# One store of eight PSUM banks, and turns by the chain of work left, in an eight-row transformer stack

## The chip, the cores and the metric

The kernel runs on one NeuronCore of a Trainium2 chip. The metric is the device time of one execution in microseconds (us), the median of several runs. The engines are TensorE (PE; its weight loads are listed as PEld), VectorE (DVE), ScalarE (ACT), GpSimd (POOL) and SyncE (SP), which issues most DMAs. PSUM is the memory that PE writes its results to, and DVE and ACT read from; it has eight banks of 512 float32 values in each of its 128 partitions.

## The reference, cut to what matters

Eight independent batch rows x[8, 256, 128] pass through four layers, each a gated attention followed by a gated feed-forward, with layer normalisation ahead of both:

```python
x = x + tanh(g_xattn[l]) * xattn_l(layernorm(x), ctx)    # l = 0..3, 256 x 256 attention
x = x + tanh(g_ffn[l])   * ffn_l(layernorm(x))
# attention l = 0, 1, 3: 16 heads of 8;  l = 2: 4 heads of 32 over one key/value head
#   l = 0 adds adj[256,256] and a mask, l = 1 has rms norms, rope and a causal mask
# ffn 0: one of 8 experts a token, 128x128;  ffn 1: 128 -> 512 -> 128 with low-rank experts, top 2
# ffn 2: one of 8 experts, 128 -> 512 with gelu, then 512 -> 128, layernorm
# ffn 3: only the tokens of rows 0 and 1 are fed (128 -> 1024 -> 128)
```

## The kernel before, in words

**Rows and lines.** The work of one batch row is cut into about 180 steps such as `("max", l, row, p)`, listed by `row_steps`. A step may have a part on several engines, in a fixed order (its `phases`). Four rows are in work at once. There are four lines: line b runs row b and then row b + 4, in order, and the four lines share all engines.

**The planner.** `Plan.place` runs on the host when the kernel is built. It walks through time with a table of durations (`COST`, with `HOP` from engine to engine and `LANDS` for DMAs) and writes out one order for each engine (`plan.orders`), which the engine then follows strictly. Whenever an engine is free, each line offers its next step on it, if what it depends on (`starts_after`) and the buffers it takes (`takes`, `psum_uses`) are there; of those that could start now, the one with the smallest `turn_of` is put next. Before, `turn_of` is the step's number in its row less the `HEAD_START` of the row: 740, 850, 700 and 699 for rows 0 to 3; 5, 40, 14 and 0 for rows 4 to 7. So every step of rows 0 to 3 goes ahead of every step of rows 4 to 7, and row 1 keeps ahead of row 0 until it is 110 steps further on.

**PSUM.** Seven banks are a common store (`BANKS`): a step takes one bank ("one") or two neighbouring ones ("two") when PE starts it, and gives them back when DVE or ACT has read them. The order says which earlier use each bank had, and PE waits for that reader's semaphore (`claim`). The eighth bank, `pv`, stands apart: it holds the weighed values of one row's attention.

**One attention.** For the wide layers (l = 0, 1, 3) eight `max` steps compute scores for row maxima: PE fills two banks, DVE reduces them (L1423; L1418 for the half-wide ones). The maxima are turned on PE (`shift_flip`, L1088), copied by ACT and sent by DMA as extra rows beside the queries. Then eight `attend` steps compute the transposed scores in two banks, DVE adds the bias in layer 0 (L1442), ACT takes exp into one of four `probs` buffers (L921, L926), POOL masks in layer 1 (L812), and after each two of them a `weigh` step multiplies the values by them into `pv` (16 PE instructions in a wide layer: float32 takes two a product). `divide` is ACT's copy of `pv` to memory (L930, its semaphore is `sums`); `o_flip` and `mix` follow (L1453 to L1461). Nearly all products are issued from one helper, L969; transposes of stacked queries and keys from L665.

**One turn.** A ring "turn" of one entry lets only one row at a time be between its first `attend` and its `sums`, in the plan; on the chip ACT's placing of the values for the attention waits for the former row's `sums` (`turn_before`), and so does PE in the first `weigh`.

Of the kernel before, what the change touches and what calls it, by code (L numbers as in the profile page):

```python
# [12 lines left out]
F32 = mybir.dt.float32  # L13
# [8 lines left out]
P = 128  # L22
BATCH = 8
# [17 lines left out]
SUBLAYERS = 8  # L41
TAIL_ROWS = 2
GROUP = 8
STACKS, WIDES, PROBS, BANKS = 3, 2, 4, 7
COLS = 32
LANES = P // COLS
SETS = HEADS // LANES
# [79 lines left out]


AHEAD = 2
HEAD_START = [740, 850, 700, 699, 5, 40, 14, 0]  # L130


COST = {"load": [("SP", .4), ("PE", .4), ("ACT", .27), ("DVE", 1.55), ("POOL", .7)], "mask": [("SP", .4)], "fetch": [("SP", .8)], "consts": [("SP", 3)],
# [29 lines left out]
LANDS = {"consts": CONSTS, "load": 4, "mask": 4, "fetch": 4, "shift_flip": 3.4, "store": 2}  # L163
HOP = {"PE": .32, "DVE": .14, "ACT": .16, "POOL": .12, "SP": .1}
# [3 lines left out]
def phases(s):  # L168

    own = COST.get(s[:2], COST[s[0]])  # L170
    if s[0] == "attend" and s[1] != 2 and s[3] == 0:
        own = [(e, us + PLACING) if e == "ACT" else (e, us) for e, us in own]
    return own
# [71 lines left out]
def takes(s, eng):  # L245

    kind, l, row = s[:3]
    out = []
    if eng == "PE":
        out += [(use, ring, until) for use, ring, until in psum_uses(s)]  # L250
    if kind == "attend" and eng == ("DVE" if l == 0 else "ACT"):
        out.append(("probs_in", "probs", ("weighed", l, row, s[3] // 2)))
    if kind == "attend" and eng == "PE" and s[3] == 0:
        out.append(("turn", "turn", ("sums", l, row)))
    if (kind, eng) == ("mask", "SP"):
        out.append(("mask", "wide", ("biasT_ps", 0, row)))
    if (kind, l, eng) in (("spread", 0, "DVE"), ("spread", 2, "DVE"), ("inner", 1, "ACT")):
        out.append(("wide", "wide", ("f_ps", l, row)))
    if (kind, eng) == ("deep", "ACT") and s[3] == 0:
        out.append(("wide", "wide", ("f_ps", 3, row)))  # L260
    if eng == "ACT" and ((kind in ("kv", "query") and l in (0, 3)) or kind in ("k_turn", "q_turn")):
        out.append((f"{kind[0]}s", "stack", (f"{kind[0]}T_ps", l, row, 1)))
    return out
# [63 lines left out]
class Plan:  # L327


    def __init__(self, rings):  # L330
# [9 lines left out]
                    self.value[(stage, *s[1:])] = count[stage]  # L340
        self.names = sorted(count)

    def place(self):

        lines = [[] for _ in range(ROWS)]
        for b in range(ROWS):
            held = None
            for row in range(b, BATCH, ROWS):
                begin, rest = row_steps(row)
# [8 lines left out]
        lines = [[s for s in line if s[0] != "next"] for line in lines]  # L358
# [4 lines left out]
        ended = {}  # L363
        slots = {ring: [0.0] * n for ring, n in self.rings.items()}
        pending, former = {}, {}
        rank = {s: b for b, line in enumerate(lines) for s in line}
        step = {}
        for row in range(BATCH):
            begin, rest = row_steps(row)
            step.update({s: n for n, s in enumerate(begin + rest)})  # L370

        def turn_of(s):

            return (step.get(s, 0) - HEAD_START[s[2]], s[2])


        def fits(ring, t=None):
# [43 lines left out]
        while todo:  # L421
            best = None
            for eng in ENGINES:
                ready = []
                for b in range(ROWS):
                    q = queues[eng, b]
                    if at[eng, b] < len(q):
                        t = earliest(q[at[eng, b]], eng)
                        if t is not None:
                            ready.append((t, q[at[eng, b]]))  # L430
                if ready:
                    now = max(clear[eng], min(t for t, _ in ready))
                    t, s = min(((t, s) for t, s in ready if t <= now), key=lambda c: turn_of(c[1]))
                    if best is None or now < best[0]:
                        best = (now, eng, s)
            now, eng, s = best
            b = rank[s]
            at[eng, b] += 1
            todo -= 1
            self.orders[eng].append(s)  # L440
            clear[eng] = ended[s, eng] = end = now + dict(phases(s))[eng]
            for use, ring, until in takes(s, eng):
                got = fits(ring, now)
                bank = "one" if ring == "two" else ring
                self.home[(use, *s[1:])] = (ring, got[0])
                self.freed_by[(use, *s[1:])] = [former[bank, i] for i in got if (bank, i) in former]
                for i in got:
                    slots[bank][i] = None
                    former[bank, i] = until
                    pending.setdefault(until, []).append((bank, i))  # L450
            for stage in signals(s, eng):
                for bank, i in pending.pop((stage, *s[1:]), []):
                    slots[bank][i] = end + HOP[eng]
# [3 lines left out]
def build(nc, dram, out):  # L457
    plan = Plan({"one": BANKS, "probs": PROBS, "wide": WIDES, "stack": STACKS, "turn": 1})

    with ExitStack() as ctx:  # L460
# [102 lines left out]
        small, rest = (t[0:3 * E, :, :].rearrange("p r n -> p (r n)") for t in (probs[2], probs[1]))  # L563

        banks = ctx.enter_context(nc.psum_tensor("banks", [P, BANKS * 512], F32))
        pv = ctx.enter_context(nc.psum_tensor("pv", [P, 512], F32))


        const_in = ctx.enter_context(nc.semaphore("const_in"))
# [7 lines left out]
        sem = {}  # L577
# [36 lines left out]
        def turn_before(l, row):  # L614

            ended = [t for t in plan.orders["ACT"] if t[0] == "divide"]
            i = ended.index(("divide", l, row))
            return ("sums", *ended[i - 1][1:]) if i else None
# [4 lines left out]
        def programs(block):  # L623
            def at(stage, s):
                return plan.value[(stage, *s[1:])]

            def bank(use, s):
                ring, i = plan.home[(use, *s[1:])]
                return banks[:, i * 512:(i + (2 if ring == "two" else 1)) * 512]

            def claim(eng, use, s):

                for stage in plan.freed_by[(use, *s[1:])]:
                    eng.wait_ge(sem[stage[0]], plan.value[stage])
# [193 lines left out]
            def _(act):  # L828
# [8 lines left out]
                for s in plan.orders["ACT"]:  # L837
                    kind, l, row = s[:3]
# [88 lines left out]
                                           scale=1.0 if l == 2 else HD ** -0.5).then_inc(sem["probs"], 1)  # L927
                    if kind == "divide":
                        act.wait_ge(sem["weighed"], at("weighed", ("weigh", l, row, SETS - 1 if l != 2 else 0)))
                        act.activation(weighed_sb[b][:, :, :], pv[:, :].rearrange("p (g q) -> p g q", g=2), ACT.Copy).then_inc(sem["sums"], 1)  # L930
                    if kind == "route" and l == 1:
                        act.wait_ge(sem["gate_in"], at("gate_in", s))
# [31 lines left out]
            def _(pe):  # L964
# [6 lines left out]
                for s in plan.orders["PE"]:  # L971
# [137 lines left out]
                    if kind == "weigh":  # L1109

                        part = s[3]
                        if part == 0:
                            if l == 2:
                                pe.wait_ge(sem["v"], at("v", ("kv", l, row)))
                            else:
                                pe.wait_ge(sem["v_placed"], at("v_placed", ("attend", l, row, 0)))
                            ended = turn_before(l, row)
                            if ended:
                                pe.wait_ge(sem[ended[0]], plan.value[ended])
                        g, j = part // 2, part % 2  # L1120
                        both = [("attend", l, row, 2 * part + i) for i in range(2)]
                        ready = "masked" if l == 1 else "probs"
# [519 lines left out]
```

## Time and profile before

| | us |
|---|---|
| median of 3 runs (lowest, highest) | 1163.98 (1162.83, 1172.91) |
| the profiled execution | 1158.67 |
| its span, first to last instruction | 1156.9 |
| PE busy / DVE busy / ACT busy / POOL busy | 938.3 / 794.3 / 501.8 / 302.9 |
| mean granted clock of TensorE | 0.838 |

The busy time of an engine is the time in which it has an instruction in work. The granted clock is a share of 2.4 GHz; its two levels in this trace are 1.0 (2.4 GHz) and 0.5 (1.2 GHz). A row of the waits says which engine and line sat idle, which instruction's semaphore ended that, for how long in all, how often, and the longest. PE takes its instructions in the written order: while it waits, all that is behind waits too.

### The profile page before, as it was taken

To read this page: it belongs to the slowest core of one execution; us is meant where nothing else is said; L and a number is where in the kernel's file an instruction comes from. 1 tells how busy PE (TensorE), PEld (TensorE's weight loads), DVE (VectorE), ACT (ScalarE), POOL (GpSimd) and SP (SyncE) were. 2 spreads that over 40 slices of the span, in tenths; PEclk is the share of its full clock that TensorE was granted. 3 is DMA by queue.
4 is the path that set the end of the run, shared out by engine and by line. 5 is a ranking of instruction groups with operands and counts; after the bars stand their busy time and mean duration, and the time that the engine had idled before them with its cause. 6 is when DMAs were issued, how large, how long until landed. Compare 5 with 4: busy or idle time off the path is not lost.

```text
span 1156.9 us, 19280 instructions
## 1 busy us (share of the span) xinstructions
PE 938.3 (81%) x7316; PEld 592.9 (51%) x7316; DVE 794.3 (69%) x1849; ACT 501.8 (43%) x760; POOL 302.9 (26%) x324
## 2 busy tenths in 40 slices
PE   4787677698998889888975887887887898998776
PEld 3442335364564467555753452355554666666533
DVE  5889888848626844856099489999786747744473
ACT  3563354352325433364082835553454234353056
POOL 3520405343123003301031221245443314010000
PEclk7787788776779889778986998797998989699969
DMA  8000000000000000000000000000000000000000
GB/s 313 15 1 2 2 2 1 1 2 1 1 2 2 2 6 11 8 2 6 1 29 2 20 19 2 1 2 1 1 4 1 1 1 2 2 1 6 0 2 16
DMA packets 11741, 14.26 MB, mean 12 GB/s; under 512 B 1604, under 2 KB 10716, under 8 KB 11396
## 3 DMA queue, kind: packets, MB, share of 16 engines
q1 hardware_dynamic: 11552, 12.88, 3.4%
q8 instruction: 61, 1.00, 0.4%
q10 hardware_dynamic: 100, 0.14, 0.1%
q14 instruction: 28, 0.23, 0.1%
HBM read 11.55 MB, written 1.05 MB: 11 GB/s over the span
## 4 chain that ended last, share of the span: by engine, by line
PE 49%; DVE 35%; ACT 8%; issue 5%; POOL 2%; DMA 1%; SPq 0%; ACTq 0%; DVEq 0%
PE banks L969 37%; DVE nm_row L1423 10%; PE pv L969 7%; DVE probs L1442 3%; PE banks L665 2%; DVE qf_row L1453 2%; ACT probs L926 2%; DVE wide L1512 2%; DVE st_row L1266 2%; DVE xn_row L1378 2%; DVE mv_row L1268 1%; POOL kss_row L759 1%; ACT qT_row L843 1%; PE banks L1023 1%; ACT probs L921 1%
## 5 line engine op out<-in xcount | busy, mean ns | idle before, releaser
L1423 DVE TENSOR_REDUCE nm_row<-banks 128x4 f32<-128x1024 f32 (+1 forms) x192 | 209.4, 1126 | 38.5 <-PE banks L969 38.0
L759 POOL TENSOR_TENSOR rstd_row<-rstd_row,neghalf 128x2 f32<-128x2 f32 x66 | 47.2, 716 | 413.4 <-DVE rstd_row L1373 297.3
L926 ACT ACTIVATE probs<-banks 128x1024 f32<-128x1024 f32 (+1 forms) x144 | 126.4, 929 | 53.4 <-PE banks L969 52.1
L969 PE MATMUL pv<-probs,vpad 128*32 128x256 f32 (+1 forms) x1536 | 111.8, 414 | 23.6 <-ACT probs L921 11.1
L969 PE MATMUL banks<-kT_row,qT_row 48*128 48x256 bf16 (+2 forms) x896 | 103.4, 328 | 32.5 <-DVE nm_row L1423 18.6
L969 PE MATMUL banks<-wide,c 128*128 128x256 f32 x512 | 126.1, 402 | 0.0
L969 PE MATMUL banks<-qT_row,kT_row 50*128 50x256 bf16 (+2 forms) x896 | 98.8, 331 | 31.6 <-ACT probs L926 7.7
L969 PEld LDWEIGHTS banks<-wide,c 128*128 128x128 f32 x512 | 99.7, 200 | 17.8 <-issue 0.7
L969 PEld LDWEIGHTS banks<-kT_row,qT_row 48*128 48x128 bf16 (+1 forms) x896 | 42.5, 121 | 100.0 <-issue 52.9
L921 ACT ACTIVATE probs<-probs 128x1024 f32<-128x1024 f32 x64 | 67.2, 1055 | 55.5 <-DVE probs L1442 53.8
L969 PEld LDWEIGHTS banks<-qT_row,kT_row 50*128 50x128 bf16 (+1 forms) x896 | 49.1, 124 | 77.4 <-issue 21.3
L969 PEld LDWEIGHTS pv<-probs,vpad 128*32 128x32 f32 x1536 | 46.8, 119 | 66.9 <-issue 34.5
L1442 DVE TENSOR_TENSOR probs<-banks,biasT_row 128x1024 f32<-128x1024 f32 x64 | 75.9, 1217 | 5.9 <-PE banks L969 5.0
L665 PE MATMUL banks<-identb,stack 128*128 128x128 bf16 x768 | 65.1, 248 | 16.6 <-DVE stack L1412 13.6
L759 POOL TENSOR_TENSOR kss_row<-kss_row,neghalf 128x32 f32<-128x32 f32 x8 | 44.4, 5544 | 116.5 <-DVE kss_row L649 116.4
L969 PE MATMUL banks<-c,wide 128*128 128x128 f32 x512 | 73.5, 304 | 0.6 <-POOL wide L817 0.6
L665 PEld LDWEIGHTS banks<-identb,stack 128*128 128x128 bf16 x768 | 55.1, 113 | 29.9 <-DVE stack L1412 18.7
L969 PEld LDWEIGHTS banks<-c,wide 128*128 128x128 f32 x512 | 68.7, 215 | 3.0 <-ACT kT_row L843 0.8
L657 ACT ACTIVATE stack<-qf_row 128x768 bf16<-128x768 f32 x48 | 40.3, 843 | 58.8 <-DVE qf_row L1387 22.1
L1378 DVE TENSOR_SCALAR xn_row<-x_row,mv_row,rstd_row 128x128 f32<-128x128 f32 x116 | 49.7, 482 | 21.0 <-POOL rstd_row L759 12.7
L953 ACT ACTIVATE wide<-banks 128x1024 f32<-128x1024 f32 x8 | 8.2, 1025 | 126.3 <-PE banks L969 126.3
L812 POOL TENSOR_SCALAR_AFFINE_SELECT probs<-probs 128x512 f32<-128x512 f32 x64 | 41.0, 654 | 80.9 <-ACT probs L926 80.3
(221 smaller groups left out, 1646.6 us busy)
## 6 DMA issues: line engine op xcount, KB each, us to landing
c<-in_c SPq DMA_DIRECT2D x1, 2500.0 KB
wide<-in_mask SPq DMA_DIRECT2D x8, 256.0 KB, 3.2
qT_row<-mT_row SPq DMA_DIRECT2D x96, 4.0 KB
c<-in_c SPq DMA_DIRECT2D x1, 1194.5 KB
xn_row<-in_ctx SPq DMA_DIRECT2D x8, 128.0 KB, 3.5
x_row<-in_x SPq DMA_DIRECT2D x8, 128.0 KB, 2.9
late<-in_late SPq DMA_DIRECT2D x2, 512.0 KB, 14.8
out<-x_row SPq DMA_DIRECT2D x8, 128.0 KB, 1.9
```

The source lines that it names most:

```text
L657: return nc.scalar.activation(stack[:, :, lo:hi, :], heads(src)[:, :, None, :].to_broadcast([P, NT * HEADS, hi - lo, HD]), ACT.Copy)
L665: ins = pe.transpose(dst[:, jj * SEQ + t * P:jj * SEQ + (t + 1) * P], src[:, hh:hh + 2, :, :].rearrange("p h g d -> p (h g d)"), identb[:, :])
L759: return pool.tensor_tensor(t, t, neghalf[:, 0:n], ALU.pow)
L812: pool.affine_select(diag, diag, [[0, 2], [0, NT], [1, P]], ALU.is_ge, 0.0, base=0, channel_multiplier=-1).then_inc(sem["masked"], 1)
L921: act.activation(dst[:, :, :], dst[:, :, :], ACT.Exp).then_inc(sem["probs"], 1)
L926: act.activation(dst[:, :, 0:w], src[:, :, 0:w], ACT.Exp, scale=1.0 if l == 2 else HD ** -0.5).then_inc(sem["probs"], 1)
L969: return pe.matmul(dst, lhsT, rhs, start=start, stop=stop, **kw)
L1266: ch.link(V.bn_stats(sums[b][:, t, :], src[:, t, :]))
L1378: ins = V.tensor_scalar(xn[b][:, t, :], x[b][:, t, :], mv[b][:, t, 0:1], rstd[b][:, t:t + 1], ALU.subtract, ALU.mult)
L1423: V.tensor_reduce(nm[b][:, t, :, 2 * jp:2 * jp + 2], ps[:, :, :, 0:kn], AX.X, ALU.max, negate=True).then_inc(sem["max"], 1)
L1442: V.tensor_tensor(held(probs, "probs_in", s)[:, :, :], bank("scores_ps", s)[:, :].rearrange("p (r n) -> p r n", r=2), bt[:, None, :].to_br ...
L1453: ch.link(V.reciprocal(over, den))
```

## The change

The `pv` tensor is gone and `BANKS` is 8. The first `weigh` of an attention takes a bank of the common store as "one", held until `sums`; all its `weigh` steps and `divide` use that bank. In the first `weigh`, PE waits for the bank's earlier reader (`claim`) in place of the former row's `sums`. ACT's `turn_before` wait and the "turn" ring stay.

The planner's turns change too. `work_left` gives each phase of each step the length of the longest chain of work of the same row that hangs on it, by the same table; along an engine the steps of a line are chained in their order. An engine now takes, of what could start, the phase with the largest sum of chain left (us) and `LEAD` of its row. The order of all engines is planned anew; no instruction is added or taken away.

```diff
-STACKS, WIDES, PROBS, BANKS = 3, 2, 4, 7
+STACKS, WIDES, PROBS, BANKS = 3, 2, 4, 8
...
-HEAD_START = [740, 850, 700, 699, 5, 40, 14, 0]
+LEAD = [274.2, 264.8, 306.7, 298.2, 14.3, 5.0, 24.2, 33.5]
...
+    if kind == "weigh" and s[3] == 0:
+        out.append(("pv_ps", "one", ("sums", l, row)))
...
+    def work_left(self, lines):
+
+        left, after = {}, {}
+        for line in lines:
+            former = {}
+            for s in line:
+                for eng, _ in phases(s):
+                    ahead = [(o, e, HOP[e] + (LANDS.get(o[0], 0) if e == "SP" else 0)) for o, e in starts_after(s, eng)]
+                    if eng in former:
+                        ahead.append((former[eng], eng, 0))
+                    for o, e, lag in ahead:
+                        if o[2] == s[2]:
+                            after.setdefault((o, e), []).append((s, eng, lag))
+                    former[eng] = s
+        for line in lines:
+            for s in reversed(line):
+                for eng, us in reversed(phases(s)):
+                    left[s, eng] = us + max([lag + left[n, e] for n, e, lag in after.get((s, eng), [])], default=0)
+        return left
...
-        def turn_of(s):
-
-            return (step.get(s, 0) - HEAD_START[s[2]], s[2])
+        left = self.work_left(lines)
+
+        def turn_of(s, eng):
+
+            return (-left[s, eng] - LEAD[s[2]], s[2])
...
-        pv = ctx.enter_context(nc.psum_tensor("pv", [P, 512], F32))
...
+                        pv = bank("pv_ps", ("weigh", l, row, 0))
                         act.activation(weighed_sb[b][:, :, :], pv[:, :].rearrange("p (g q) -> p g q", g=2), ACT.Copy).then_inc(sem["sums"], 1)
...
-                            ended = turn_before(l, row)
-                            if ended:
-                                pe.wait_ge(sem[ended[0]], plan.value[ended])
+                            claim(pe, "pv_ps", s)
+                        pv = bank("pv_ps", ("weigh", l, row, 0))
```

## Rows read from the trace of the kernel before

**Rows 1.** The page: its span, and each engine's busy us, share and instructions.
```profile
span 1156.9 us, 19280 instructions
PE 938.3 (81%) x7316; PEld 592.9 (51%) x7316; DVE 794.3 (69%) x1849; ACT 501.8 (43%) x760; POOL 302.9 (26%) x324
```
**Rows 2.** The page: the chain that ended last, shares of the span by engine.
```profile
PE 49%; DVE 35%; ACT 8%; issue 5%; POOL 2%; DMA 1%; SPq 0%; ACTq 0%; DVEq 0%
```
**Rows 3.** Busy us of each engine by stretch; granted clock, DMA share, GB/s.
```profile
50.00:200.00 150.00, 112.44 (x974) 59.77 (x973) 131.18 (x246) 71.90 (x98) 42.67 (x26) 0.81 0.01 2
200.00:350.00 150.00, 128.35 (x873) 81.16 (x872) 90.32 (x246) 50.93 (x90) 49.52 (x54) 0.75 0.01 1
350.00:600.00 250.00, 211.79 (x1568) 146.83 (x1564) 146.92 (x375) 109.14 (x162) 49.03 (x68) 0.88 0.03 8
600.00:850.00 250.00, 199.28 (x1753) 112.58 (x1749) 212.04 (x450) 123.80 (x179) 87.94 (x67) 0.82 0.02 6
850.00:1050.00 200.00, 178.49 (x1327) 122.28 (x1320) 125.54 (x348) 83.90 (x144) 47.38 (x72) 0.89 0.01 2
1050.00:1157.00 107.00, 79.64 (x665) 50.23 (x663) 53.62 (x90) 41.52 (x54) 4.29 (x6) 0.86 0.02 6
```
**Rows 4.** Waits of PE: us in total, times, longest us; five of its groups.
```profile
PE banks L969 <- DVE nm_row L1423: 31.5, 53, 2.3
...
PE banks L969 <- ACT probs L926: 9.9, 19, 1.8
PE banks L969 <- DVE probs L1442: 9.4, 13, 2.5
...
PE banks L969 <- DVE qf_row L1365: 5.6, 2, 5.4
...
PE banks L969 <- DVE nm_row L1418: 2.5, 2, 1.9
```
**Rows 5.** Five short stretches of `max` steps, columns as in rows 3, and their sum.
```profile
36.50:46.50 10.00, 7.84 (x56) 2.79 (x55) 9.43 (x10) 2.13 (x6) 3.81 (x3) 1.00 0.11 34
...
613.00:628.00 15.00, 8.04 (x56) 3.33 (x57) 15.00 (x15) 0.23 (x1) 0.00 (x0) 0.65 0.01 1
...
sum 59.00, PE 43.83 PEld 16.07 DVE 56.50 ACT 12.70 POOL 3.81; mean PE 8.77 PEld 3.21 DVE 11.30 ACT 2.54 POOL 0.76
```
**Rows 6.** The page's groups: the reduction behind each `max` step, busy and mean ns.
```profile
L1423 DVE TENSOR_REDUCE nm_row<-banks 128x4 f32<-128x1024 f32 (+1 forms) x192 | 209.4, 1126 | 38.5 <-PE banks L969 38.0
```
**Rows 7.** The tile `pv`: its copy by ACT, and who waited for it.
```profile
L930 ACT ACTIVATE biasT_row<-pv x32: 597/597/618, 67.3 to 1149.0; 128x512 f32<-128x512 f32 x32
...
  ACT biasT_row L930: 48.1, 27
  DVE qf_row L1453: 25.8, 7
  PEld banks L969: 3.4, 6
  PE banks L969: 1.5, 3
```
**Rows 8.** Timeline of SP: the stores of rows 1, 5 and, last, three rows.
```profile
460.28 0.41 SPq L733 DMA_DIRECT2D out<-x_row  x1
...
1064.01 0.42 SPq L733 DMA_DIRECT2D out<-x_row  x1
...
1136.32 18.70 SPq L733 DMA_DIRECT2D out<-x_row  x3
```
**Rows 9.** Two stretches with PE nearly always busy, columns as in rows 3.
```profile
545.00:600.00 55.00, 49.13 (x317) 38.48 (x315) 22.77 (x52) 21.74 (x26) 5.88 (x7) 0.99 0.05 15
...
269.00:292.00 23.00, 21.74 (x109) 10.45 (x107) 19.83 (x57) 6.59 (x12) 5.43 (x3) 0.51 0.01 1
```

More of the change, by code:

```diff
@@ L366, in place @@
         rank = {s: b for b, line in enumerate(lines) for s in line}
[L367 to L370, printed above, removed]
-        def turn_of(s):
-            return (step.get(s, 0) - HEAD_START[s[2]], s[2])
+        left = self.work_left(lines)
+        def turn_of(s, eng):
+            return (-left[s, eng] - LEAD[s[2]], s[2])
         def fits(ring, t=None):
@@ L432, in place @@
                     now = max(clear[eng], min(t for t, _ in ready))
-                    t, s = min(((t, s) for t, s in ready if t <= now), key=lambda c: turn_of(c[1]))
+                    t, s = min(((t, s) for t, s in ready if t <= now), key=lambda c: turn_of(c[1], eng))
                     if best is None or now < best[0]:
```

## The prediction

> **What bounds the kernel now.** I read the page first. PE is busy for 938.3 us of 1156.9 and DVE for 794.3 [rows 1]; no other engine is near. PE is thus idle for 1156.9 - 938.3 = 218.6 us, and as the change neither adds nor takes away an instruction, it can gain only from these 218.6 us, or from PE's clock. The chain that ended last runs over PE for 49% of the span and over DVE for 35% [rows 2]: neither engine bounds alone. The busy time by stretch says when each does [rows 3]. From 50 to 200 us, when all four first rows are in their first layer, DVE is busy for 131.18 us of 150 (87%) and PE for 112.44 (75%). From 200 to 600 us PE leads, with 340.1 of 400 (85%). From 600 to 850 us, where rows of the second half begin, DVE is again ahead with 212.04 of 250 (85%) beside 199.28 (80%). From 850 to 1050 us PE is busy for 178.49 of 200 (89%, the best), and the last 107 us fall back to 79.64 (74%). So the kernel alternates between stretches set by DVE and stretches set by PE. A better order would put the PE work of one row beside the DVE work of another.
>
> The waits of PE tell what a bank is worth [rows 4]. PE fills banks that somebody must have read before. Five of its groups end with such a reader: 31.5 us for the reduction of the maxima (53 times), 9.9 for exp, 9.4 for the bias, 5.6 and 2.5 for two others, 58.9 us in all. Part of the 9.9 may be a wait for data, so I count 58.9 as the most that banks can cost PE by these rows.
>
> **Part 1, the eighth bank.** A wait for a bank has two possible causes: too few banks, or a reader that can't keep up. Five stretches of `max` steps, 59 us together, tell them apart: PE is busy for 43.83 us and DVE for 56.50 [rows 5]. PE is idle for 15.2 us of them, DVE for 2.5. In the one from 613 to 628 us DVE is busy for all 15.00 us and PE for 8.04. A reduction takes 1126 ns [rows 6] and PE has the next two banks full before that; with a fourth pair of banks PE gets ahead by one more step and then waits as before. What the bank takes away at once is at most DVE's own idle share, 2.5 of 15.2, which on the 58.9 us is 9.7 us. Beyond that, the step that PE runs ahead shortens a later stretch only if PE sets that one. There are 24 wide attentions; at one `max` step of PE each, worked out as 7.84 us of PE over 8 steps and other work [rows 5], so under 0.98 us, this is under 23.5 us, and I take an eighth of it, 3 us, since the bank is not free whenever values are being weighed and the next stretch is often DVE's. The term is -12.7 us, between 0 and -58.9.
>
> A rule speaks for more: the Trainium skill, Perfetto Trace Analysis, section Matmul Optimizations, says that all eight PSUM banks should be used so that instructions can overlap. Here all eight are used already, one of them for `pv` alone; the trace agrees with the rule only so far as the reader has time left. By the rule the term would be the whole -58.9 us, by the stretches above -9.7 us.
>
> **Part 2, the wait of the first `weigh`.** Removed: PE's wait for the former `sums`. No row of PE's waits has `pv` waiting for L930; the waits for that copy are ACT's own for its input and those of what reads the result [rows 7]. It stood behind the "turn", which stays. So nothing is gained. Added: a claim of one bank, 32 times. What is queued behind it is the `weigh` (16 matmuls) and then everything on PE. If no bank is read yet, the wait is up to one reduction, 1.126 us [rows 6], so 32 x 1.126 = 36 us at the worst. The plan starts the `weigh` only where it expects a bank, and three short waits are as much as I'd expect to go wrong: +2 us, between 0 and +36. The copy itself stays as it is, 32 times 597 ns [rows 7]. DMAs are unchanged in number; their issue moves with their steps, on a queue with nothing else to do.
>
> **Part 3, the order of turns.** The old order keeps row 1 far ahead: it is stored at 460.28 us and its line's second row, row 5, at 1064.01 us; the other three lines end together, with their stores between 1136.32 and 1155.0 us [rows 8]. So the last 93 us have three rows in place of four, and PE is idle for 27.4 us of the last 107 [rows 3]. The new order gives the turn to the longest chain left plus a lead. The leads of the first four rows differ by 42 us and those of the last four by 28.5, so the four lines are held within some 40 us of chain of each other, and all run nearly to the end. Suppose the last 107 us reached the idle share of the stretch before (21.5 of 200, 10.8%): 11.5 us idle, a gain of 15.9. But the end of any last row is a bare chain (exp, weigh, divide, spread, mix), and about half of the gain is lost to it: -8 us. In the middle, 600 to 850 us has 50.7 us of PE idle (20%). Begun together, the second rows would be like the first in 50 to 200 us, 25% idle; for 150 us that is 37.6 us against 30.4 at the present share: +7 us. In exchange the first rows finish together, none waits for its line, and the PE-heavy second layers of the feed-forward can be laid beside others' attention by chain length rather than by step number, which counts a step of 15 us in the planner's table like one of 0.4 us. I can't price this from a row; the bound is the difference between the idle share of the whole (218.6 of 1156.9, 18.9%) and the best stretch (10.8%), 8.1% of 1156.9 = 94 us below, and to the share of the first 150 us (25%), +71 us above. Between ends so far apart I take the sixth part of the gain way that a better measure of urgency may bring, -9 us, nearer to no change because DVE-set stretches stay. The sum of part 3 is -8 + 7 - 9 = -10 us.
>
> **The clock.** The mean grant is 0.838. The Trainium skill, TensorE: Matmul & The Clock Gate, section The HAM clock gate, ties 2.4 GHz to a busy PE, so a denser order would be rewarded. Here the rows disagree: from 545 to 600 us PE is busy for 49.13 of 55 at 0.99, but from 269 to 292 us it is busy for 21.74 of 23 at 0.51, the low level [rows 9]. So I price the clock at nothing. By the rule, with the cost of the low level at most 938.3 x (1 - 0.838) = 152 us and the idle time down by a tenth, it would be up to 15 us more gain.
>
> **Sum.** 1156.9 - 12.7 + 2 - 10 = 1136.2 us of span. The profiled execution was 1.8 us longer than its span, and the median of the runs is 5.3 us above the profiled one, so 1136.2 + 1.8 + 5.3 = 1143.3; I say 1142 us, 1.9% under 1163.98.
>
> **Rivals.**
> Rival A, banks are the bound: all 58.9 us of rows 4 go, with the order's -10: 1156.9 - 58.9 - 10 + 7.1 = 1095 us; a half of it still gives 1124. For it: waits for readers are a quarter of PE's idle time. Against: DVE is busy for 96% of the stretches where they fall.
> Rival B, nothing comes of it: what PE gets ahead is given back to DVE, whose 794.3 us lie in the same places, and the end is a bare chain anyhow. 1164 us, within 1% either way. For it: the two engines share the last chain nearly evenly.
> Rival C, lockstep, on the slower side: the lines kept within 40 us of chain bring all four rows to the same DVE-heavy layer at once, as in 50 to 200 us, and the far-ahead row 1 that now fills the gaps is lost. If the 25% idle share of that stretch holds for 250 us more than now, in place of 18.9%, the cost is 250 x 0.061 = 15 us; with no gain from part 1 the time is 1179 us. It decides once PE is idle for more than about 230 us in all. For it: the first 150 us are just this case. Against: the leads keep the rows some 10 us apart, and the "turn" forces a further distance.
> By these: my forecast 0.50, A 0.12, B 0.22, C 0.16. About 1% is what a measurement of this kernel can tell from no change; a tenth of my own case falls within it. Faster by over 1%: 0.45 + 0.12 = 0.57. Within 1%: 0.22 + 0.05 = 0.27. Slower by over 1%: 0.16. The range runs from a half of rival A with a little more from the order, 1110 us, to rival C's 1179; the forecast's own range is 1120 to 1155.
>
> **What the next profile would show.** Right: PE busy within some 15 us of 938 and its idle time near 198 us; the waits of PE for L1423 down by about a fifth, not gone, with DVE still near 96% busy in the `max` stretches; no noticeable wait of the first `weigh`; four stores in the last 40 us or so; PE busy above 80% in the last 107 us. A is right if waits for the readers fall below 20 us. C is right if the first 200 us and those around 600 us have PE under 75%. The forecast is wrong if PE's idle time stays at 219 us, if the mean clock moves by over 0.03 (it would outweigh part 1), or if banks taken one at a time by `weigh` split the pairs, so that waits of `max` and `attend` steps grow.

## The result, and the profile after

The changed kernel takes 1084.42 us (median of 4 runs, 1081.33 to 1086.0) where the kernel before took 1163.4 us beside it (4 runs). The ratio is 0.930, with a 95% interval of 0.925 to 0.936: 7.0% faster. The forecast was 1142 us with a range down to 1110; the direction was right, and the size was off by a factor of three and a half (79 us for 22).

The page of the changed kernel begins with its span and the busy time of each engine (us, share, instructions), as in [rows 1]:

```profile
span 1081.3 us, 19274 instructions
...
PE 887.4 (82%) x7316; PEld 572.0 (53%) x7316; DVE 793.3 (73%) x1849; ACT 493.2 (46%) x753; POOL 302.5 (28%) x324
```

PE has the same 7316 instructions, yet its busy time fell by 938.3 - 887.4 = 50.9 us. Its idle time fell from 218.6 to 1081.3 - 887.4 = 193.9 us, by 24.7. So of the 75.6 us of span two thirds came out of PE's busy time, which the prediction priced at nothing, and one third out of idle time, which is all that it priced. PE did not get less work: it is the clock, whose mean grant is 0.894 against 0.838. Busy time times mean grant, an estimate of the work in us at the full clock, is 786 us before and 793 after. The other executions agree: their grants are 0.875 to 0.894 for the changed kernel and 0.826 to 0.847 for the kernel before. With two levels, a mean of 0.838 puts PE at the low one for 32% of the span, 375 us; a mean of 0.894 is 21%, 229 us. DVE's busy time did not move (794.3 and 793.3 us).

Stretches of the changed kernel, with the columns of [rows 3] (busy us of PE, PEld, DVE, ACT, POOL; granted clock; DMA share; GB/s):

```profile
50.00:200.00 150.00, 119.61 (x998) 69.51 (x998) 137.06 (x276) 72.97 (x97) 43.22 (x25) 0.83 0.01 2
200.00:350.00 150.00, 126.81 (x1094) 80.49 (x1092) 112.95 (x301) 65.56 (x130) 63.96 (x76) 0.90 0.01 2
350.00:600.00 250.00, 223.92 (x1763) 151.52 (x1755) 165.53 (x377) 116.06 (x163) 43.66 (x57) 0.92 0.04 12
600.00:850.00 250.00, 197.16 (x1772) 116.75 (x1770) 212.40 (x504) 120.75 (x185) 97.13 (x87) 0.86 0.01 2
850.00:1050.00 200.00, 177.69 (x1303) 127.37 (x1301) 122.85 (x292) 79.08 (x122) 31.42 (x47) 0.92 0.01 2
...
974.30:1081.30 107.00, 81.53 (x767) 48.69 (x764) 64.48 (x105) 53.40 (x71) 4.19 (x6) 0.85 0.02 7
```

The reader should compare the first five stretch by stretch with [rows 3]. PE is busy for 119.6 us from 50 to 200 us, not 112.4, and the clock is higher in all five: 0.90 for 0.75 from 200 to 350 us, 0.92 for 0.88 and for 0.89 in the third and the fifth. From 600 to 850 us, where the second rows begin, DVE is still ahead with 212.4 us of 250. The last row is the last 107 us, as long as the last row of [rows 3]: PE is idle for 25.5 us of them, where it was 27.4.

SP's stores tell when each row ends, as in [rows 8]:

```profile
525.42 0.39 SPq L751 DMA_DIRECT2D out<-x_row  x1
536.66 0.41 SPq L751 DMA_DIRECT2D out<-x_row  x1
572.19 0.41 SPq L751 DMA_DIRECT2D out<-x_row  x1
595.97 0.42 SPq L751 DMA_DIRECT2D out<-x_row  x1
...
1048.68 10.62 SPq L751 DMA_DIRECT2D out<-x_row  x2
1069.02 10.36 SPq L751 DMA_DIRECT2D out<-x_row  x2
```

The first four rows end within 71 us of each other and are all out at 596 us; the last four are stored between 1048.7 and 1079.4 us. Before, one line ended at least 72 us ahead of the others.

Three of PE's waits for a bank's reader, as in [rows 4]:

```profile
PE banks L988 <- DVE nm_row L1441: 37.6, 56, 2.3
...
PE banks L988 <- DVE probs L1460: 12.2, 19, 1.1
...
PE banks L988 <- ACT probs L944: 9.4, 21, 1.0
```

They did not shrink, with one bank more: 59.2 us where the same three groups had 50.8.

And by shape, the float32 products of layer 2's attention, first of the kernel before, then of the changed one (count | busy us, mean ns | idle before them):

```profile
L969 PE MATMUL banks<-qT_row,kT_row 34*128 34x256 f32 x128 | 26.0, 561 | 0.5 <-DVE nm_row L1423 0.5
L969 PE MATMUL banks<-kT_row,qT_row 33*128 33x256 f32 x128 | 24.5, 525 | 3.1 <-DVE nm_row L1423 1.7 <-DVE nm_row L1418 0.7 <-ACT qT_row L896 0.4
...
L969 PE MATMUL pv<-probs,v_row 128*32 128x256 f32 x128 | 14.6, 540 | 2.6 <-ACT probs L926 2.6
```

```profile
L988 PE MATMUL banks<-qT_row,kT_row 34*128 34x256 f32 x128 | 17.8, 398 | 0.4 <-ACT kT_row L861 0.4
L988 PE MATMUL banks<-kT_row,qT_row 33*128 33x256 f32 x128 | 17.2, 391 | 0.0
...
L988 PE MATMUL banks<-probs,v_row 128*32 128x256 f32 x128 | 10.1, 384 | 1.1 <-ACT probs L944 0.8 <-issue 0.3
```

Same shapes, same counts, 540 ns before and 384 after: in the kernel before most of layer 2's attention ran at the low level, in the changed one next to none of it. The rows of these three groups are 20.0 us shorter together, beside the 50.9 us of all PE work.

### The profile page after: what moved, and what is told of

It reads as the page before. It is cut to its first block, busy times and chain, and to the rows that moved or that the text cites. A ratio compares the mean times of both kernels' runs of the same rounds, so it can differ in the third digit from the quotient of the medians.

```text
span 1081.3 us, 19274 instructions
## 1 busy us (share of the span) xinstructions
PE 887.4 (82%) x7316; PEld 572.0 (53%) x7316; DVE 793.3 (73%) x1849; ACT 493.2 (46%) x753; POOL 302.5 (28%) x324
## 4 chain that ended last, share of the span: by engine, by line
PE 45%; DVE 39%; ACT 7%; issue 6%; SPq 1%; DMA 1%; POOL 1%; DVEq 0%; ACTq 0%
PE banks L988 41%; DVE nm_row L1441 11%; DVE probs L1460 4%; ACT probs L944 3%; DVE wide L1530 2%; PE banks L683 2%; DVE qf_row L1471 2%; DVE st_row L1284 2%; DVE mv_row L1286 1%; DMA xn_row<-in_ctx 1%; DVE xn_row L1396 1%; DVE oh_row L1506 1%; DVE stack L1430 1%; DVE qr_row L1426 1%; PE banks L1042 1%
## 5 line engine op out<-in xcount | busy, mean ns | idle before, releaser
L1441 DVE TENSOR_REDUCE nm_row<-banks 128x4 f32<-128x1024 f32 (+1 forms) x192 | 211.8, 1129 | 55.5 <-PE banks L988 55.0
L988 PE MATMUL banks<-probs,vpad 128*32 128x256 f32 (+1 forms) x1536 | 108.1, 402 | 14.0 <-ACT probs L939 7.0
L988 PE MATMUL banks<-qT_row,kT_row 50*128 50x256 bf16 (+2 forms) x896 | 90.1, 300 | 29.1 <-DVE nm_row L1441 13.6
L988 PE MATMUL banks<-kT_row,qT_row 48*128 48x256 bf16 (+2 forms) x896 | 95.0, 303 | 19.1 <-DVE nm_row L1441 12.6
L988 PE MATMUL banks<-c,wide 128*128 128x128 f32 x512 | 78.6, 317 | 2.7 <-POOL wide L835 2.3
L988 PEld LDWEIGHTS banks<-kT_row,qT_row 48*128 48x128 bf16 (+1 forms) x896 | 37.2, 110 | 82.1 <-issue 49.8
L988 PEld LDWEIGHTS banks<-qT_row,kT_row 50*128 50x128 bf16 (+1 forms) x896 | 40.8, 110 | 71.9 <-issue 30.1
L988 PEld LDWEIGHTS banks<-c,wide 128*128 128x128 f32 x512 | 72.6, 226 | 7.2 <-issue 4.9
L988 PEld LDWEIGHTS banks<-probs,vpad 128*32 128x32 f32 x1536 | 45.8, 116 | 55.0 <-issue 26.2
L683 PEld LDWEIGHTS banks<-identb,stack 128*128 128x128 bf16 x768 | 52.8, 109 | 25.0 <-DVE stack L1430 14.7
L861 ACT ACTIVATE qT_row<-banks 128x1024 bf16<-128x1024 bf16 x48 | 47.4, 1022 | 31.9 <-PE banks L683 31.5
```

The costliest lines, as they stand in the source:

```text
L683: ins = pe.transpose(dst[:, jj * SEQ + t * P:jj * SEQ + (t + 1) * P], src[:, hh:hh + 2, :, :].rearrange("p h g d -> p (h g d)"), identb[:, :])
L861: act.activation(dst, cols, ACT.Copy, **kw).then_inc(sem[stage], 1)
L988: return pe.matmul(dst, lhsT, rhs, start=start, stop=stop, **kw)
L1441: V.tensor_reduce(nm[b][:, t, :, 2 * jp:2 * jp + 2], ps[:, :, :, 0:kn], AX.X, ALU.max, negate=True).then_inc(sem["max"], 1)
```

## The experiments

The change has two parts, the bank and the turns, and the second has three things in it: the measure (chain left in place of step number), the spread of the four rows (near even in place of one far ahead), and the choice of one set of eight numbers, which settles one order among many. Theory T says that the turns made the gain, theory S the bank. Each kernel builds its orders with the planner in it; that planner's own end is quoted with each run. It is the figure of a table, not a measurement, and the last of the tables below sets it beside the chip. Only the lines of an edit that matter are shown; `...` stands for what is left out.

### The two parts alone: e1 and e2

e1 is the changed kernel with the old turns:

```diff
-LEAD = [274.2, 264.8, 306.7, 298.2, 14.3, 5.0, 24.2, 33.5]
+HEAD_START = [740, 850, 700, 699, 5, 40, 14, 0]
...
-            return (-left[s, eng] - LEAD[s[2]], s[2])
+            return (step.get(s, 0) - HEAD_START[s[2]], s[2])
```

> The eight-bank store alone; turns by step number with the old leads. Theory T (the turns made the gain): no change, 1150 to 1172 us, PE idle about 215 us and granted clock about 0.84. Theory S (the bank made it, rival A of the prediction): at least half of the 79 us, so under 1124 us. The kernel's planner, by its own table, ends at 1078.7 us where the kernel before has 1077.0.

e2 is the kernel before with the new turns, `pv` apart and seven banks:

```diff
-HEAD_START = [740, 850, 700, 699, 5, 40, 14, 0]
+LEAD = [274.2, 264.8, 306.7, 298.2, 14.3, 5.0, 24.2, 33.5]
...
-            return (step.get(s, 0) - HEAD_START[s[2]], s[2])
+            return (-left[s, eng] - LEAD[s[2]], s[2])
```

> Turns by the chain left plus the new leads, pv apart and seven banks as before. Theory T: at least three quarters of the 79 us, so under 1105 us, with the clock near 0.89. Theory S: over 1124 us. A third, that each needs the other (a bank pays only when rows are close together), expects something between, and e1 without gain. The planner ends at 1049.5 us, against 1017.3 for the changed kernel.

e1 took 1153.8 us, 0.995 of the kernel before (0.992 to 0.997). e2 took 1115.6 us, 0.958 (0.953 to 0.963). Their busy times:

```profile
span 1151.3 us, 19281 instructions
...
PE 930.8 (81%) x7316; PEld 597.7 (52%) x7316; DVE 794.0 (69%) x1849; ACT 501.3 (44%) x761; POOL 302.6 (26%) x324
```

```profile
span 1123.9 us, 19277 instructions
...
PE 916.7 (82%) x7316; PEld 582.1 (52%) x7316; DVE 789.1 (70%) x1849; ACT 501.7 (45%) x757; POOL 303.1 (27%) x324
```

The bank alone is worth about 7.5 us under the old turns (0.3 to 0.8%); S falls. None of it shows as idle time in the profiled executions: PE is idle for 1151.3 - 930.8 = 220.5 us in e1, against 218.6 before, and its waits for the three readers did not fall but rose, from 50.8 to 68.7 us:

```profile
PE banks L991 <- DVE nm_row L1444: 39.8, 46, 2.9
PE banks L991 <- DVE probs L1463: 20.3, 15, 6.3
...
PE banks L991 <- ACT probs L947: 8.6, 16, 1.5
```

The turns alone are worth 46 us and not the 59 that T asked for. In the profiled execution of e2, the slowest of its five (1125.6 us beside a median of 1115.6), idle time is 11.4 us less than before and PE's busy time 21.6 us less. 7.5 + 46 is 53 of 79 us, so the two together give more than their sum, as the third theory has it. That each is worth more with the other is not shown by this: the leads of e1 and e2 were not chosen for their rule and number of banks, and the choice of leads alone moves the time by 20 to 40 us (e8 and e11 below).

### Which part of the turns: e3, e4 and e5

e3 keeps the step number and the eight banks, and gives the first four rows leads within 42 steps of each other; e4 does the same to the kernel before, with seven banks and `pv` apart:

```diff
-HEAD_START = [740, 850, 700, 699, 5, 40, 14, 0]
+HEAD_START = [679.8, 713.9, 706.8, 671.8, 40.1, 34.9, 50.6, 28.0]    # e3
+HEAD_START = [670.9, 713.9, 704.0, 679.5, 61.4, 35.3, 50.6, 26.4]    # e4
```

> Eight banks, turns by step number as before, but with leads of the first four rows within 42 steps of each other (679.8, 713.9, 706.8, 671.8; 40.1, 34.9, 50.6, 28.0) in place of 151. Splits theory T: if it was the even start of the rows, this comes within 25 us of the changed kernel, 1085 to 1110 us; if it was the measure (chain left and not step number), it stays over 1130 us. The planner ends at 1035.5 us.

> The kernel before with nothing changed but its eight leads (670.9, 713.9, 704.0, 679.5; 61.4, 35.3, 50.6, 26.4): seven banks, step numbers, rows that start nearly even. If the even start is the main cause, 1115 to 1145 us and a clock over 0.86; if bank or measure is needed for it, 1150 us or more. The planner ends at 1060.1 us.

e3 took 1113.7 us, 0.958 (0.953 to 0.963); e4 1135.4 us, 0.977 (0.972 to 0.982). So eight numbers in the kernel before, and nothing else, give 26 us, and the eighth bank, with leads of its own, gives 22 more. e4's time is what the even start asked for, its mean grant of 0.859 just short of the 0.86. e3 lands just outside the 1085 to 1110 us of the even start, far from the 1130 of the measure. Yet the measure has a price too: from e3 to the changed kernel, both with eight banks and near-even rows, it is 29 us, and with seven banks, from e4 to e7 below, 19 us. Spread 26, bank 22 and measure 29 add up to the 77 to 79 us, with one order standing for each kernel. e3 and the changed kernel have the same idle time of PE (1111.2 less 918.3 us busy is 192.9, against 193.9); they differ in PE's busy time, 918.3 and 887.4.

e5 is the changed kernel with row 1 far ahead:

```diff
-LEAD = [274.2, 264.8, 306.7, 298.2, 14.3, 5.0, 24.2, 33.5]
+LEAD = [274.2, 424.8, 306.7, 298.2, 14.3, 5.0, 24.2, 33.5]
```

> The changed kernel with one number altered: row 1 leads by 160 us more (264.8 to 424.8), so that it runs far ahead as in the kernel before. If the near-even start carries a large part of the gain, 1110 to 1135 us; if chain length and bank are enough in whatever spread, it stays under 1095 us. The planner ends at 1056.4 us (1017.3 for the changed kernel).

It took 1132.1 us, 0.974 (0.970 to 0.978): 48 us of the 79 are lost by one number, within the range of the even start. But e8 below loses 38 us with no row sent ahead, so only some 10 of the 48 us are more than one small move of the leads cost. That a far-ahead row costs time rests on e4 more than on e5. Rival C of the prediction had rows kept close together as a cost, and neither run shows one.

### How much is the rule, and how much the one order: e8, e11, e12

A lead moved by a little gives other orders throughout. By the planner, sets of leads drawn within 3 us of the new ones end between about 1030 and 1080 us, with a median near 1050, where the changed kernel has 1017.3. Sets within 2 steps of the old ones end between about 1080 and 1115 us, with a median near 1097, where the kernel before has 1077.0. Both kernels are thus at the good end of their neighbourhoods. e8 and e11 take a middling neighbour of each, e12 a good order from leads elsewhere:

```diff
+LEAD = [275.6, 265.5, 305.0, 298.3, 16.7, 3.4, 27.0, 33.8]     # e8, the changed kernel otherwise
+HEAD_START = [739, 849, 700, 699, 7, 39, 14, 1]                # e11, the kernel before otherwise
+LEAD = [255.1, 245.8, 279.7, 289.6, 20.0, 10.8, 30.5, 39.2]    # e12, the changed kernel otherwise
```

> The changed kernel with each lead moved by at most 2.8 us (275.6, 265.5, 305.0, 298.3, 16.7, 3.4, 27.0, 33.8). A theory by which the gain comes from the rule (chain left, near-even rows, eight banks) expects 1075 to 1095 us, as the rule is the same. A theory by which a good part comes from the choice of one good order among many expects 1110 to 1125 us: the planner ends at 1052.0 us in place of 1017.3, and the chip has so far been 66 to 84 us above the planner.

> The kernel before with each of its leads moved by at most 2 steps (739, 849, 700, 699; 7, 39, 14, 1). What e8 asks of the new rule, asked of the old: if its leads had been as well chosen, this is slower by about as much as the planner says (1097.5 us against 1077.0), 1170 to 1190 us. If orders of the old rule are all much the same, 1155 to 1168 us.

> The changed kernel with other leads, of another place altogether, for which the planner ends at 1015.9 us (255.1, 245.8, 279.7, 289.6; 20.0, 10.8, 30.5, 39.2). If the planner's end tells the chip's to some 10 us, 1075 to 1095 us, as the changed kernel. If 1084 us was luck of one order on the chip, 1100 us or more.

e8 took 1122.2 us, 0.965 (0.961 to 0.969); e11 1184.3 us, 1.018 (1.011 to 1.024); e12 1078.4 us, 0.927 (0.922 to 0.932). Spans and PE of e8 and e11:

```profile
span 1120.7 us, 19278 instructions
...
PE 911.3 (81%) x7316; PEld 584.2 (52%) x7316; DVE 790.8 (71%) x1849; ACT 492.8 (44%) x753; POOL 302.7 (27%) x324
```

```profile
span 1189.6 us, 19277 instructions
...
PE 962.8 (81%) x7316; PEld 610.8 (51%) x7316; DVE 789.7 (66%) x1849; ACT 496.9 (42%) x757; POOL 303.3 (25%) x324
```

Moving no lead by more than 2.8 us costs 38 us, about half the gain. From one middling order to the other, e11 to e8, rule and bank together are worth 62 us; the choice was worth about 22 us to the old kernel and 38 to the new, and the difference of 16 makes up the 78. One order stands here for each neighbourhood, so the split may be off by 10 us or more: e11 and e8 were picked as middling by the planner, not by the chip.

The planner can say what a middling order of the other kernels would be, if 100 or so sets are drawn around their leads in the same way: about 1089 us for e1, 1090 for e4, 1071 for e3, 1074 for e5 and 1067 for e7. In its table, then, the bank is worth 8 or 9 us under the old leads, 19 with near-even rows and step numbers and 17 with the chain left; the even start by itself 7, the measure 21, and a far-ahead row costs 24. These are figures of a table, not of the chip. e12 shows that the good time is not bound to one set of leads. It beats the kernel before by 7.3%; its interval overlaps that of the changed kernel, so whether it is better than that one is not settled.

### The bank under the new rule: e7 and e9

e7 is e2 with leads that suit seven banks. e9 is the changed kernel with the store cut to seven, the weighed values still in it:

```diff
+LEAD = [256.0, 266.1, 296.4, 287.0, 35.4, 26.0, 45.8, 42.5]    # e7
...
-STACKS, WIDES, PROBS, BANKS = 3, 2, 4, 8
+STACKS, WIDES, PROBS, BANKS = 3, 2, 4, 7                       # e9
```

> As e2 (turns by chain left, pv apart, seven banks), but with leads that suit seven banks (256.0, 266.1, 296.4, 287.0; 35.4, 26.0, 45.8, 42.5), for which the planner ends at 1040.0 us in place of 1049.5. It tells how much of the 31 us between e2 and the changed kernel is the bank's, and how much that its leads were chosen for eight. If the bank's: 1108 to 1116 us as e2; if the choice: 1095 us or less.

> The changed kernel, its leads too, with seven banks in the store in place of eight, the weighed values still among them; so the store is one bank smaller than ever. The bank's worth in this rule, all else the same: if banks matter little (as the prediction had it, some 13 us) 1090 to 1100 us; by the planner, which ends at 1052.9 us and not at 1017.3, 1115 to 1130 us.

e7 took 1116.4 us, 0.962 (0.957 to 0.967); e9 1125.7 us, 0.967 (0.961 to 0.973). e7 is no better than e2, so with `pv` apart the chip stays at 1116 us with either set, and the shared eighth bank is worth 31 to 32 us to the new rule. That is four times the 7.5 us of e1, but e1's leads were chosen for seven banks, so the two can't be set side by side; e4 to e3, each with leads of its own, gives 22. A bank less in the store costs 41 us, but the leads were those for eight, and a part of the 41 is that choice. Of e9's waits for a bank's reader the same three groups as above are:

```profile
PE banks L988 <- DVE nm_row L1441: 42.8, 63, 3.2
PE banks L988 <- ACT probs L944: 18.0, 32, 1.8
PE banks L988 <- DVE probs L1460: 17.2, 24, 2.4
```

78.0 us with seven banks and 59.2 with eight, by the same rule and leads: here the waits do fall, by 19 us. PE's idle time falls from 1125.7 - 919.6 = 206.1 to 193.9, and its busy time from 919.6 to 887.4.

### The clock: e6 and e10

These two experiments add work to PE and nothing else. e6 adds two large products ahead of the real ones in layer 2 of the kernel before, e10 one ahead of each `max` step of the wide layers in e9, into the unused bank, at a place where PE soon waits for DVE:

```diff
+                        if l == 2:                                   # e6, after the claims of max and attend
+                            stir(bank("max_ps", s), 2)           # and the same for "scores_ps"
...
+                        if l != 2:                                   # e10, ahead of the claim of max
+                            mm(spare[:, :], identb[:, :], trib[:, None, :].to_broadcast([P, 4, P]), skip_group_check=True)
```

> The kernel before with its order, and two bfloat16 products of 128 x 128 by 128 x 512 added ahead of the real ones in each max and attend step of layer 2, into the banks just claimed, where the real ones overwrite them: 64 products more, at some 0.21 to 0.43 us each 14 to 28 us of PE work. It asks what sets the clock in layer 2, where the float32 products on 33 or 34 partitions ran at 525 and 561 ns in the kernel before and at 391 and 398 ns after. If the clock follows how much of the array the work uses, those products fall toward 400 ns, the mean clock rises over 0.85, and the time is within 10 us of the kernel before in spite of the added work. If it follows something else (the idle gaps of PE, or chance), they stay near 540 ns and the kernel is 10 to 25 us slower.

> As e9, with one bfloat16 product of 128 x 128 by 128 x 512 ahead of the claim of each max step in layers 0, 1 and 3 (192 in all, 0.22 us each at the high level, 41 us), into the bank that e9 leaves unused; PE does them where it would soon wait for DVE. It asks if idle PE in these stretches is what lowers the clock. If so the mean clock rises by 0.03 or more over e9's, other products get shorter, and the time is within 1% of e9's or below it. If idle time is not the cause, the clock stays and the kernel is 20 to 40 us slower.

e6 took 1181.9 us, 1.016 (1.010 to 1.022), with a mean grant of 0.834 where the kernel before has 0.838. Of layer 2's products, those on 34 partitions went from 561 to 470 ns and those that weigh the values from 540 to 462, but those on 33 from 525 to 541. So most of them did get shorter, none down to the 384 to 398 ns of the changed kernel, and the clock of the whole did not rise. The result fits neither branch, and what sets the clock in layer 2 stays open.

e10 took 1120.2 us, 0.963 (0.956 to 0.971), with 192 products more than e9, which took 1125.7. Its mean grant is 0.901 against 0.869. First e9, then e10:

```profile
span 1125.7 us, 19277 instructions
...
PE 919.6 (82%) x7316; PEld 584.2 (52%) x7316; DVE 793.0 (70%) x1849; ACT 498.1 (44%) x755; POOL 302.4 (27%) x324
...
L988 PE MATMUL banks<-wide,c 128*128 128x256 f32 x512 | 131.2, 414 | 0.0
...
L988 PE MATMUL banks<-probs,vpad 128*32 128x256 f32 x1280 | 106.9, 447 | 15.1 <-ACT probs L939 5.9 <-ACT probs L944 3.3 <-issue 2.4
```

```profile
span 1119.1 us, 19661 instructions
...
PE 935.1 (84%) x7508; PEld 583.7 (52%) x7508; DVE 792.9 (71%) x1849; ACT 499.1 (45%) x755; POOL 301.9 (27%) x324
...
L989 PE MATMUL banks<-wide,c 128*128 128x256 f32 x512 | 125.4, 400 | 0.0
L989 PE MATMUL banks<-probs,vpad 128*32 128x256 f32 x1280 | 101.0, 427 | 15.9 <-ACT probs L940 6.5 <-ACT probs L945 2.8 <-issue 2.6
L989 PE MATMUL spare<-trib,identb 128*128 128x512 bf16 x192 | 78.9, 411 | 4.3 <-ACT qT_row L862 4.3
```

The reader should see that work that has nothing to do with the added products got shorter (414 to 400 ns, 447 to 427). PE's busy time rose by only 15.5 us. Busy time times mean grant, which is 799 us in e9, is 843 in e10, so the added work is some 43 us at the full clock, and the faster clock gave back most of what it costs. (The 78.9 us of its own row count each product from start to end, also where the next one has begun.) PE's idle time fell from 206.1 to 184.0 us. The grants of the four executions are 0.862 to 0.871 in e9 and 0.901 to 0.916 in e10. With the same order, then, idle PE in these stretches lowers the clock, and filling it raises it by some 0.03 to 0.04. The added products are also large ones, but e6 adds the same kind where PE has little idle time (6.2 us ahead of the three groups of layer 2 shown above), and its mean grant does not rise. As a means it gives nothing sure: the ranges of e9 and e10 overlap.

### The planner's end beside the chip

| kernel | planner's end, us | chip, median us | PE busy, us | PE idle, us | granted clock |
|---|---|---|---|---|---|
| e12 | 1015.9 | 1078.4 | 883.4 | 195.7 | 0.895 |
| changed | 1017.3 | 1084.4 | 887.4 | 193.9 | 0.894 |
| e3 | 1035.5 | 1113.7 | 918.3 | 192.9 | 0.869 |
| e7 | 1040.0 | 1116.4 | 907.8 | 202.4 | 0.872 |
| e2 | 1049.5 | 1115.6 | 916.7 | 207.2 | 0.865 |
| e8 | 1052.0 | 1122.2 | 911.3 | 209.4 | 0.868 |
| e9 | 1052.9 | 1125.7 | 919.6 | 206.1 | 0.869 |
| e5 | 1056.4 | 1132.1 | 912.3 | 216.4 | 0.868 |
| e4 | 1060.1 | 1135.4 | 926.0 | 207.0 | 0.859 |
| before | 1077.0 | 1163.4 | 938.3 | 218.6 | 0.838 |
| e1 | 1078.7 | 1153.8 | 930.8 | 220.5 | 0.845 |
| e11 | 1097.5 | 1184.3 | 962.8 | 226.8 | 0.813 |

The last three columns are of the profiled execution, and PE idle is span less busy; for e2 and e11 that execution was the slowest, 10 and 7 us over the median. Over twelve kernels with the same PE instructions the idle time goes from 193 to 227 us and PE's busy time, by and large, with it, from 883 to 963, while busy time times grant stays between 783 and 799 us. So PE's busy time is set by the clock. The planner ranks them nearly as the chip does: 81.6 us apart in its table are 105.9 us on the chip. The table has one duration a step; that on the chip the order also changes how long each product takes is a likely reason for the wider spread.

## Why the prediction was wrong, point by point

**Direction and bound.** Right: the gain is in PE's idle time and PE's clock, as the first paragraph had it, and DVE's work is unchanged.

**The clock: 0 us, the step that failed.** The terms of the sum are all idle time, -12.7 + 2 - 10 = -20.7 us, and idle time fell by 24.7 us. PE's busy time, held at 938 us, fell by 50.9 to 887.4 because the mean grant rose by 0.056; this term is 50.9 of the 75.6 us of span, and without it the measured time would have been near the forecast. The prediction refused the term on the strength of one stretch, 269 to 292 us, busy at the low level [rows 9]. That row shows that a busy PE may stay at the low level for long; it says nothing of how PE got there. The same trace, just ahead of it:

```profile
263.00:269.30 6.30, 3.16 (x30) 1.83 (x26) 6.16 (x14) 0.26 (x1) 5.64 (x10) 1.00 0.00 0
269.30:303.40 34.10, 32.84 (x174) 15.67 (x175) 23.43 (x65) 9.13 (x16) 5.13 (x3) 0.50 0.01 1
```

PE is busy for half of 6.3 us at the high level, beside a DVE that is busy for 6.16, and the low level that follows holds for 34 us in which PE is busy all but 1.3. Another fall, also of the kernel before:

```profile
612.50:617.40 4.90, 2.26 (x21) 1.07 (x20) 4.87 (x6) 0.73 (x2) 0.00 (x0) 1.00 0.02 3
617.60:641.00 23.40, 14.26 (x96) 6.45 (x100) 18.42 (x39) 6.68 (x10) 6.91 (x3) 0.50 0.01 2
```

PE is busy for 2.26 of 4.90 us beside a DVE that is busy for 4.87, and the next 23 us are at the low level. All but the first 0.5 us of these 4.9 lie in the stretch from 613 to 628 us of [rows 5], which the prediction read for idle time alone. The Trainium skill, TensorE: Matmul & The Clock Gate, section The HAM clock gate, has the clock follow how busy PE has been; e10 bears that out with the order unchanged. The 34 us above show that a busy PE alone does not bring the high level back soon. By that rule the prediction had named 15 us, from idle time down by a tenth; idle time fell by 11%, and the clock gave three times as much.

The amount of idle time does not settle the clock: e3 has the idle time of the changed kernel (192.9 and 193.9 us) and 31 us more of busy time. Its trace enters the low level 42 times, that of the changed kernel 31 times and that of the kernel before 37 times. It is not the long waits either: idle times of PE of over 1 us add up to 102 us in e3 and 112 us in the changed kernel, 50 in each. Which property of the order it is, and why layer 2's attention runs at the high level in the changed kernel, stays open.

**Part 1, the bank: -12.7 us, mis-sized and near in e1 by luck.** Under the old turns e1 gives -7.5 us, but not in the way that was argued: idle time is 1.9 us more and the waits for readers 18 us more, where the term was to take both down. With near-even rows idle time falls by 14.1 us (e4 to e3), 8.5 (e7 to the changed kernel) and 12.2 (e9 to it), about as forecast, and the time by 22, 32 and 41 us, since PE's busy time falls as well. Right is that DVE is the one that PE waits for and that such waits stay (59.2 us after). The five stretches of [rows 5] hold 15.2 us of PE's idle time and were made to stand for waits of 58.9. The rule of the Trainium skill (Perfetto Trace Analysis, Matmul Optimizations: use all eight banks) comes out between: not the 58.9 us of all such waits, and they do not vanish, but more than the forecast. Where the bank pays is only partly shown: 19 us less of waits for readers from e9 to the changed kernel, and the rest through the order that it makes possible.

**Part 2, the wait of the first `weigh`: +2 us, right in kind.** No large group of PE's waits belongs to it, and e1, which has it, lost no time. It was not measured by itself.

**Part 3, the turns: -10 us, near as idle time, by luck.** e2 has 11.4 us less idle time, but gives -46 us, for the same reason of the clock. The pieces did not come out. The better end (-8) was to leave 19 of the last 107 us idle; it is 25.5 for 27.4, -2. The worse start of the second rows (+7) is 52.8 us idle from 600 to 850 us for 50.7, +2. The -9 was a guess, and misnamed: a sixth of the 94 us is 15.7, and 9 is a tenth (with 15.7 the forecast would have been 1137 us). The +7, and with it rival C, rested on reading 50 to 200 us as what close rows cost. e4 gives -26 us by making the rows nearly even, 11.6 us of it idle time. That the first 150 us were poor also in the kernel before was no evidence on spread, since there all lines begin together under any leads; in the changed kernel the same stretch has PE busy for 119.6 us and not 112.4, with DVE at 91%.

**The signs.** Idle time is 193.9 us where 198 was named, and four stores lie in the last 33 us; DVE is still busy for 80.75 of 85 us in five stretches of `max` steps. Against the forecast, PE's busy time is 51 us off and not within 15, the wait for the reduction behind `max` rose from 31.5 to 37.6 us in place of falling by a fifth, and PE is busy for 76% of the last 107 us and not 80. Two of the three signs by which the forecast called itself wrong appeared: the clock moved by over 0.03, and the waits of `max` and `attend` steps grew, though not shown to be for the reason given there. Rival A, with 1095 us, came nearest to the measured 1084, for a reason that did not hold, as the waits for readers did not go.

**The choice of the order.** The prediction had no term for it at all. e8 and e11 put it at 38 us for the new kernel and 22 for the old, 16 net of 79.

Added up: rule, spread and bank, taken between middling orders, 62 us; the better choice 16 us. In the profiled executions of e11 and e8, PE's busy time is 51.5 (962.8 to 911.3) of the 68.9 us between their spans; between e8 and the changed kernel it is 23.9 (911.3 to 887.4) of 39.4: most of either reaches the time through the clock.

## What to carry to other kernels

When a change makes an order anew, look at what the clock does after the stretches in which TensorE waits, and do not price the idle time alone; here the clock gave twice what the idle time gave. A busy stretch at the low level is no evidence that waits do not matter: look at what stands ahead of it. A wait that is the reader's fault in the present order says what a bank is worth in that order only. Where orders come from a list scheduler, compare middling orders of two rules before crediting a rule with the time of its best one: a lead moved by under 3 us cost half of this gain.

## What the runs showed of the hardware

192 products more, placed where TensorE would wait, made the kernel no slower (1120.2 us beside 1125.7), with the mean grant up from 0.869 to 0.901 and unrelated products 3 to 5% shorter. In layer 2 of the kernel before, 64 large products added beside small ones did not lift the clock of the whole (0.834 beside 0.838), though most of that layer's products got shorter. Over twelve orders of the same work TensorE's busy time went from 883 to 963 us, and busy time times mean grant stayed between 783 and 799. The clock can fall to the low level after a stretch in which TensorE is only half busy (3.16 of 6.30 us) and stay there through 34 us in which it is busy for 32.84.
